# Attention stages: each group of four gathers is waited for before the next one is issued

## What is computed

```
x = x + 0.5 * moe(layernorm(x))      # layer 0
x = x + attention(layernorm(x))
x = x + 0.5 * moe(layernorm(x))      # layer 1, same weights
```

## Time and profile before

| | us |
|---|---|
| median of 3 runs (lowest, highest) | 1988.15 (1980.69, 1991.82) |
| the profiled execution, its own time | 1987.23 |
| its span in the trace | 1985.5 |
| PE, PEld busy | 1483.1 (75%), 1248.2 (63%) |
| DVE busy | 1046.6 (53%) |
| POOL busy | 836.3 (42%) |
| ACT busy | 617.9 (31%) |

### The profile page before, as it was taken

How to read it: one execution, slowest core, us unless ns; L and a number is a source line. 1 busy time by engine, 2 the same in 40 slices (tenths; PEclk the granted TensorE clock), 3 DMA queues, 4 the chain that set the end, 5 groups by cost and what they waited for, 6 DMA issues and landing times.

```text
span 1985.5 us, 35564 instructions
## 1 busy us (share of the span) xinstructions
PE 1483.1 (75%) x11274; PEld 1248.2 (63%) x11275; DVE 1046.6 (53%) x3253; ACT 617.9 (31%) x1254; POOL 836.3 (42%) x1060
## 2 busy tenths in 40 slices
PE   4797787999966878578676877699665547799760
PEld 4796686988854558446564557598544326688550
DVE  4666556644434655557645567244346547384332
ACT  2333223444432323223222323144222112244220
POOL 4553585565532200130083003756333442755646
PEclk9897898999986988779787898799767777899885
DMA  3722323556552112220232012255422443346555
GB/s 117 228 86 78 93 80 108 167 167 158 164 143 59 39 54 86 80 59 23 74 115 69 25 36 84 84 162 161 132 64 74 137 128 105 100 146 163 154 166 177
DMA packets 175218, 215.71 MB, mean 109 GB/s; under 512 B 18800, under 2 KB 156144, under 8 KB 175088
## 3 DMA queue, kind: packets, MB, share of 16 engines
q0 software_dynamic: 28416, 77.63, 14.9%
q1 hardware_dynamic: 100976, 92.32, 14.4%
q10 hardware_dynamic: 45696, 44.05, 6.8%
HBM read 119.56 MB, written 94.37 MB: 108 GB/s over the span
## 4 chain that ended last, share of the span: by engine, by line
PE 54%; DVE 16%; issue 11%; POOL 6%; another core or an unknown queue 6%; ACT 5%; DMA 1%; ACTq 0%; DVEq 0%; POOLq 0%; SPq 0%
PE bank L1468 8%; PE bank L1479 7%; PE bank L1618 7%; PE bank L1480 6%; PE bank L1481 6%; PE bank L1539 4%; POOL queries_high L763 2%; DVE bn_stats L1066 2%; DVE score_maxima L1352 2%; PE bank L1870 2%; PE bank L1813 2%; ACT raw_weights L907 1%; PE bank L1697 1%; DVE score_maxima L1409 1%
## 5 line engine op out<-in xcount | busy, mean ns | idle before, releaser
L746 POOL DMA_INDIRECT rows_and_results<-normalised_by_token,rows_of_slots x336 | 319.3, 950 | 223.2 <-PE bank L1468 134.7
L689 POOL DMA_INDIRECT gathered_results<-slot_results,slot x128 | 121.7, 951 | 389.8 <-DVE combined_rows L1302 282.0
L1250 DVE TENSOR_TENSOR rows_transposed_low<-bank,rows_transposed_high 128x512 fp32r<-128x512 f32 x168 | 116.0, 691 | 268.2 <-ACT rows_transposed_high L836 173.5
L1479 PE MATMUL bank<-expert_gate_up_high,rows_transposed_high 128*128 x672 | 211.3, 314 | 32.4 <-DVE rows_transposed_low L1250 17.4
L761 POOL TENSOR_SCALAR keys_high<-iota,place_in_page_of_choice 128x128 fp32r<-128x128 f32 x96 | 58.0, 604 | 339.6 <-DVE place_in_page_of_choice L1189 332.2
L1480 PE MATMUL bank<-expert_gate_up_low,rows_transposed_high 128*128 x672 | 194.7, 290 | 2.6 <-issue 2.6
L1481 PE MATMUL bank<-expert_gate_up_high,rows_transposed_low 128*128 x672 | 193.5, 288 | 0.0
L1618 PE MATMUL bank<-expert_down,hidden_work 128*128 x672 | 185.3, 400 | 2.6 <-issue 2.0
L1479 PEld LDWEIGHTS bank<-expert_gate_up_high,rows_transposed_high 128*128 128x128 f32 x672 | 132.6, 197 | 46.8 <-issue 45.2
L1479 PE MATMUL bank<-rows_transposed_high,shared_gate_up_high 128*128 128x256 f32 x512 | 160.1, 313 | 0.3 <-DVE hidden_work L1025 0.3
L1480 PE MATMUL bank<-rows_transposed_low,shared_gate_up_high 128*128 128x256 f32 x512 | 153.7, 300 | 0.0
(11 more groups left out here) (275 smaller groups left out, 3694.0 us busy)
## 6 DMA issues: line engine op xcount, KB each, us to landing
slot_results<-rows_and_results ACTq DMA_DIRECT2D x168, 256.0 KB
partial_sums<-rows_and_results SPq DMA_DIRECT2D x96, 256.0 KB, 2.1
rows_and_results<-partial_sums SPq DMA_DIRECT2D x72, 256.0 KB, 3.1
normalised_by_token<-normalised_rows SPq DMA_DIRECT2D x64, 256.0 KB, 2.5
rows_and_results<-in_L_attn_hidden_states SPq DMA_DIRECT2D x32, 256.0 KB, 3.2
normalised_rows<-partial_sums SPq DMA_DIRECT2D x24, 256.0 KB
out<-normalised_rows SPq DMA_DIRECT2D x24, 256.0 KB
rows_and_results<-normalised_by_token,rows_of_slots POOLq DMA_INDIRECT x336
```

What stands on the lines that cost most here:

```text
L689: gp.indirect_dma_start(into[:, t, k, :], None, ys[part], bass.IndirectOffsetOnAxis(ap=slot[:, b, k, 2 * i + t:2 * i + t + 1], axis=0))\
L746: gp.indirect_dma_start(rows[:, i % NS, t, :], None, norm_d, bass.IndirectOffsetOnAxis(ap=listed[:, page:page + 1], axis=0))\
L1250: dve.tensor_tensor(flat(xt_l[:, k]), bank[k][:], flat(xt_h[:, k]).bitcast(F32), ALU.subtract)\
L1479: pe.matmul(out_, lh, rh, start=first, stop=False)
```

## The change

After the four indirect DMAs of a group, GpSimd waits until the group's own semaphore shows all four as landed, in `gather` always, in `last_pair` where the stage is an A stage.

```diff
@@ last_pair
                 gather_pair(last_gath[n % 2], last_in[n % 2], 1, last["b"], n % PB)
+                if ph["kind"] == "A":
+                    gp.wait_ge(last_in[n % 2].sem, (l - n % 2) * 32 + 64)
@@ gather
                     gather_pair(gath[:, c % 2], gathered[c % 2], 0, ph["b"], i)
+                    gp.wait_ge(gathered[c % 2].sem, (c - c % 2) * 32 + 64)
                     if ph["last"] and i >= 4:
                         for n in range(2 * i - 8, 2 * i - 6):
                             last_pair(ph, n)
```

## The result

The changed kernel takes 1937.18 us (median of 4 runs, 1932.32 to 1941.60); the kernel before, run beside it, 1989.99 us. The ratio is 0.974, with a 95% interval of 0.972 to 0.977. So the change wins 2.6%, some 53 us. The forecast of 1969 us had the sign, and the wide range (1926 to 2003) held the result, but the forecast's own range (1950 to 1978) did not: it had 19 us of gain where there are 53.

What follows compares the result with a forecast made beforehand. The prediction took PE's near standstill during long gather runs as the bound. Terms +2.7 +1.7 -7.5 -3.5 -4.6 -8 gave -19.2 us, so 1969 us; the forecast's own range was 1950 to 1978, the wide range 1926 to 2003.

Steps and rivals of the forecast that it cites:

- What bounds the kernel: A stages: PE's dense, small matmuls nearly stand still during a long run of gathers, until it has landed; mechanism unknown.
- The waits added: POOL's gather groups: 1.7 us more for each group followed by another, 6.7 instead of 5.0; ordinary A stages cost nothing.
- Batch 2's start: Start of batch 2's A stage: group 1 lands 0.9 us late, groups 2 and 3 cost 1.8; together +2.7 us.
- A4's runs of 12: A4's two cycles of 24.4 and 27.5 us: third group lands after 20.1 us, slack used up, no cost or win.
- POOL as A4's last bound: End of A4: ten groups from 1561.3 take POOL 67 us, so the stage ends at about 1630 at best.
- I take -2.5 each: Self attentions of batches 0 to 2: less crawl as gaps break up the runs, -7.5 us in all.
- -3.5 in A4: A4's self attention: breaking up its run of 16 gathers wins 3.5 us.
- the prediction's two bounds: Stall taken away: below, nothing won; above, all remote waits of A stages go, but for about 1.5 us each.
- A4's runs of 8 and 16: Later A4: two cycles of 8 win 4.6 us, the last 16 win 8, one later landing at the end costs 1.7.
- All of the crawl goes: Rival, chance 0.17: the self attentions' and A4's end's crawl all goes, -67 us, about 1921 us.
- It evens out: Rival, chance 0.22: data in flight alone hold PE, four as 16 do; costs of +4.4 against small gains, 1985 to 1993 us.
- Slower: Rival, chance 0.22: waits lengthen each run and PE crawls throughout, with no recovery in gaps; about +37, 2025 us.

Runs made afterwards that it cites:

- padded plain transfers: Kernel before with each indirect gather replaced by a plain transfer of 128 consecutive rows, three small memsets after each; 1863.03 us (0.935).
- twos: Changed kernel with a wait after every two gathers instead of after every four; 1965.83 us (0.987).

## Why the prediction was right in sign and wrong in size

**What bounds the kernel: right.** ACT's remote waits were PE's crawl under runs of gathers, and they went with the runs. The padded plain transfers show it by itself: same packets, same pace, no crawl. The prediction left the cause open and took data in flight for its sums; the runs say that it is the issuing.

**The waits added: right in the ordinary stages, short in A4.** 1.7 us a group was forecast, and the groups stand 7.0 us apart instead of 5.0. They cost nothing in ordinary stages (ready(5) at 653.54 needs no wait), as said. Batch 2's start costs +1.0 of the +2.7. A4's runs of 12 cost 2.3 us by VectorE's starts (1511 to 1532, -42.3 to -40.0), where 0 was forecast: ready(6)'s slack was used up as said, but the third group was taken at 1489.52, 21.9 us after POOL's first issue at 1467.66, not 20.1, and DVE waited 11.93 us for it. So the 6.7 us a group was short. POOL as A4's last bound: right. DVE's last sum waits 4.76 us for it, to 1600.13. DVE at ready(6), then POOL at the end:

```profile
1489.52 0.88 DVE L1300 SCALAR_TENSOR_TENSOR rows_and_results<-gathered_results,weights,rows_and_results 128x256 f32<-128x256 f32 x2 [11.93 <-DMA gathered_results<-slot_results,slot]
```

```profile
1584.87 1.14 POOL L689 DMA_INDIRECT normalised_rows<-slot_results,slot  x1 [2.44 <-DMA gathered_last_results<-slot_results,slot]
...
1593.54 0.94 POOL L689 DMA_INDIRECT gathered_last_results<-slot_results,slot  x1 [3.77 <-DMA normalised_rows<-slot_results,slot]
...
1597.35 0.95 POOL L689 DMA_INDIRECT gathered_last_results<-slot_results,slot  x1 [0.30 <-issue]
```

A group takes up to 8.7 us here, and ten groups from 1522.92 on take 74 us to the start of the last issue alone, where the prediction had 67 for all.

**The step that failed: "I take -2.5 each", -7.5 for three self attentions, and -3.5 in A4.** They measured -7.4, -6.2, -7.6 and -10.8: 32 us instead of 11. The mechanism (gaps let PE go on) was right, and this term of the sum was far too small. By the prediction's own count, some 3 us of crawl in each 6.7 us and all but the first 3 us of a run, three groups give 9 us of crawl for 14 before, a win of 5; it set the 17 us of the whole run against the 20 us of stop and go instead, and took 2.5. In the trace PE loses less again: ACT's remote waits in batch 0's stage are 3.41 and 3.86 us, where one of 13.83 stood. The padded plain transfers win 16.6 us in batch 0's self attention, about what the whole crawl was worth there, so the changed kernel keeps some 9 us of it, and the forecast let 14.5 stay. Half way between the prediction's two bounds, 6.3 us, would have been near for batches 0 to 2 (7.1 on average) and low for A4. The choice near the lower end had no row behind it.

**A place left out: the ends of two expert stages, -4.7 and -5.4.** The prediction took its runs from the A stages' windows. It named groups 0 and 1 only in batch 2's stage; those of batch 0 and of A4 go out in the expert stage before, at the end of runs of ten (554.69 to 565.96, and 1389.20 to 1400.48). With the 21 of the self attentions that makes 31 us; by VectorE's starts 28.6 were missing (47.8 less 19.2), since A4's other terms came out smaller than forecast.

**A4's runs of 8 and 16.** -4.6 and -8 +1.7 were forecast; measured are 0.0 (1532 to 1595) and -5.0 (1595 to 1664). Two groups take 15 to 16 us there (1539.00 to 1554.71 on POOL), not 13.4, and that is hardly less than the cycles of 17.0 and 16.6 before. (The -4.6 is itself off: 17.0 + 16.6 less 2 x 14.7 is 4.2.) With the self attention's larger gain, A4 came to 211.5 us where 212 was forecast: two errors that met, so luck. Batch 2's stage, forecast "as now", is 6.4 us shorter.

**The rivals.** *All of the crawl goes* (-12.5 for each self attention) fell for fours, but is what twos bring: 13.2, 11.6 and 12.8 us. Its total came nearer than the forecast; its terms add up to -65, 1923 us, and not to the -67 and 1921 given. The objection to it, that landing follows the last issue by as much after 12 as after 4, fits what the runs say, that the data isn't the matter. *It evens out* stood on data in flight alone. Half the bytes changed nothing, and plain transfers of all of them did no harm: false. *Slower* needed that PE gets less than 1.7 us of full speed out of each gap; it gets more, and wins even from pauses of 0.9 us. The Trainium skill's rule in "DMA: Bandwidth & Descriptors", section "Rules for kernel authors" (issue early, wait late), pointed the wrong way here, but the waits themselves aren't what wins: pauses without any wait for data win more.

## What to carry to other kernels

When TensorE has many small instructions and another engine's releases show up as "remote" or unknown waits, lay GpSimd's timeline beside them: a run of indirect DMAs slows TensorE for as long as it lasts. Break such runs into twos with about 1 us of anything between where GpSimd has time to spare, and pause by fours where GpSimd is the next bound (by twos with a landing each, A4 lost 28.8 us). Count every run that reaches into a neighbouring stage, and price a stall from rows at both ends, here a long run and a single group, and not by a guess near one of them.

## What was not expected of the hardware

- An indirect gather of 64 rows takes POOL 0.90 us and one of 128 rows 0.95; a plain transfer of the 128 takes 0.54. Half the bytes or half the indices take the crawl away in no part that could be told, and the time changes by 0.4% at most.
- In a run of indirect DMAs 1.25 us apart PE starts one or two matmuls a microsecond (6 and 9 in 5 us, rows above), while VectorE works on in the first of these stretches (3.40 us busy) and has nothing to do in the second. At 1.5 us apart it had 84 in 5 us. On plain transfers of the same packets from the same queue it isn't slowed. The Trainium skill, "DMA: Bandwidth & Descriptors", section "SWDGE vs HWDGE vs iDMA", says that for both kinds of GpSimd's DMAs, direct and indirect, software there computes the descriptors; by the runs here only the indirect kind slows TensorE, so having them computed there is not enough for it.
- By what path GpSimd's indirect issue slows TensorE, no run here shows. That other engines with as many small instructions would suffer too wasn't tried.
